# Feed-forward tiles of 1024 tokens in three passes, where they had 512 tokens in two

## The chip, the cores and the metric

One core of a Trainium2 chip. The time is the device time of one execution of the whole program, in microseconds; three executions are shown and their median counts.

## What is computed

A transformer block on 64 x 128 = 8192 tokens of width 512, all in float32.

```
x = x + tanh(g_xattn) * attention(layernorm(x), ctx, ctx)      # 32 query heads, 8 key heads, per batch of 128 tokens
n = layernorm(x)
shared = (silu(n @ Wsg) * (n @ Wsu)) @ Wsd * sigmoid(n @ Wse)  # 512 -> 1408 -> 512, every token
routed = for each of 32 experts: its first 64 tokens by top-4 choice,
         (silu(xe @ Wg) * (xe @ Wu)) @ Wd, weighted, added to their tokens   # 512 -> 352 -> 512
x = x + tanh(g_ffn) * (shared + routed)
```

## The kernel before

**Two stages.** The attention stage works through the 64 batches and writes the new rows to the output, the normalized rows and their transpose (`xT_dram`) to DRAM; beside that it prepares the first shared weights. The feed-forward stage, to which the change belongs, starts at 714.7 us in the profile and lasts to the end.

**Precision.** Every product of the shared part is made of three fast products: high x high, high x low, low x high (L1401 to L1403 and L1424 to L1426). So each operand exists as a rounded high part and a low part. ScalarE (ACT) writes the high part by a copy, VectorE (DVE) or GpSimd (POOL) the low part by a subtraction.

**Loops.** The 1408 hidden columns are 11 chunks of 128. They are covered in two passes over all tokens, of 5 and then 6 chunks (`NF`), since the split weights of one pass fill the memory that there is. A pass runs over 16 tiles of 512 tokens (`TILE`). A tile has a step for each chunk and then a down part.

**A step** multiplies both up projections of the chunk with the tile at once, by one level of a Strassen-Winograd scheme: seven products instead of eight, named by their operands (A11 B11, A12 B21, S4 B22, A22 T4, S2 T2, S1 T1, S3 T3). Each has two halves of depth and three precisions, so 42 matmuls per step, of 256 columns (`HT`, half a tile). They go to `p_a`, `p_b` and `p_c` in PSUM. ACT and DVE move and add the sums while TensorE (PE) goes on: ACT copies `p_a` and `p_c` to `term` and `sum16` (L1137, L1142, L1145); DVE adds them (L1357, L1319, L1364); ACT takes the silu (L1115); DVE multiplies the two halves of the tile (`h1`, L1322, and `h2`, L1325); ACT makes the high part `hh` (L1122) and DVE the low part `hl` (L1332). The last two products of a step, S4 B22 and A22 T4 (`last_two`, L1406), are issued inside the next step; those of the last step of a tile are issued inside the down part.

**The down part** (`down`, L1413) multiplies each block of 128 tokens with the down weights of the tile's chunks: three matmuls of 512 columns per chunk and block, into one of two banks of `acc`. DVE adds each finished block to its row of the output (`add_acc`, L1334). PE may write block j only when DVE has added block j - 2. Between these additions DVE prepares the next tile: four sums of its blocks (`x_sum`, L1189) and seven low parts (`x_low`, L1194), each over 512 elements per partition; ACT makes the seven high parts (`split_x`, L1100). The order in which PE takes the chunks of block 0 is written out by hand at L1479 to L1486: the last chunk's product has to wait for the whole chain from A22 T4 to `hl`, and other products are put ahead of it.

**Experts.** The 32 experts are done in 16 pairs, one pair beside one tile: gather of the rows (POOL), four transposes, 32 matmuls for gate and up, three transposes (L1466), six matmuls (L1473). The results are added to the output rows by gather, addition (L1284) and scatter, for each of the two halves; this may begin when the rows of the tile before have been stored (L1061), and the rows of the running tile may be loaded only after it (L957).

**Queues.** SP issues all plain loads and stores in the order of the program; its waits hold up what is behind them. Each engine works in the order of its code.

```
 31 NF = (5, 6)
 35 TILE = 512
1476 end = T.nf - 1
1480 down(T, 0, range(0, 2))
1481 last_two(T, end)
1482 down(T, 0, range(2, end))
1484 down(T, 1, range(0, 2))
1485 down(T, 0, range(end, T.nf))
1486 down(T, 1, range(2, T.nf))
```

## Time and profile before

| | us |
|---|---|
| median of 3 executions (2277.85 to 2278.27) | 2277.96 |
| the profiled execution | 2276.01 |
| its span, first to last instruction | 2274.2 |
| busy: PE / DVE / ACT / POOL | 2192.4 / 1539.9 / 1178.4 / 651.8 |
| feed-forward stage, first shared product to last | 714.7 to 2271.0 |
| granted TensorE clock, mean | 0.994 |

A matmul on PE overlaps the next one, so its duration in a row is longer than the time that it takes from the engine. What counts is the distance from start to start. A wait shows as a gap, or as a longer distance. In the rows, `chosen` also holds `gate`, `act_g`, `sum16`, `up2` and `eo`, since these share its memory, `x_raw` also holds the four sums, and `top` holds `xeT` and `y0`.

### The profile page before, as it was taken

How to read it: one execution, taken by the hardware profiler on the slowest of the kernel's cores; microseconds unless marked ns; L12 is line 12 of the kernel's file. 1: busy time of each engine (PE TensorE's matmuls, PEld its weight loads, DVE VectorE, ACT ScalarE, POOL GpSimd, SP SyncE). 2: the span in 40 equal slices, each digit the busy share in tenths (PEclk: the TensorE clock that was granted, in tenths of full speed). 3: DMA queues.
4: the chain of work that ended last, by engine and by line, in shares of the span. 5: the costliest groups of instructions: out<-in, count | busy, mean ns of one | idle time of the engine just before them, and what ended most of it. 6: DMA issues, size and time to landing. Idle time of an engine off the chain costs nothing. (4 is left out here: it accounts for less than half of the span.)

```text
span 2274.2 us, 53961 instructions
## 1 busy us (share of the span) xinstructions
PE 2192.4 (96%) x17121; PEld 1842.6 (81%) x17121; DVE 1539.9 (68%) x3135; ACT 1178.4 (52%) x2363; POOL 651.8 (29%) x1553
## 2 busy tenths in 40 slices
PE   6999999999997999999999999899999999999999
PEld 4777777777775888988889888798988989888888
DVE  6999999999996886556556556665555545455554
ACT  5888888888885433333333343433333333333332
POOL 5777777777773100000000003200000100001000
PEclk9999999999998999999999999999999999999999
DMA  3555555555554213443434435324243334344431
GB/s 82 144 141 139 147 142 134 147 143 136 143 151 125 68 65 129 147 147 110 143 120 138 141 116 174 130 96 137 84 138 92 115 101 137 98 153 157 155 104 65
DMA packets 318827, 286.25 MB, mean 126 GB/s; under 512 B 123265, under 2 KB 236929, under 8 KB 318722
## 3 DMA queue, kind: packets, MB, share of 16 engines
q1 hardware_dynamic: 314370, 272.23, 39.5%
q0 software_dynamic: 4352, 12.65, 2.1%
q8 instruction: 62, 1.02, 0.2%
q14 instruction: 43, 0.35, 0.1%
HBM read 195.43 MB, written 88.34 MB: 125 GB/s over the span
## 5 line engine op out<-in xcount | busy, mean ns | idle before, releaser
L1401 PE MATMUL p_a<-x_h,ws_h 128*128 128x256 f32 x1280 | 377.2, 295 | 17.3 <-ACT term L1137 10.1
L1402 PE MATMUL p_a<-x_l,ws_h 128*128 128x256 f32 x1280 | 363.0, 284 | 0.0
L1403 PE MATMUL p_a<-x_h,ws_l 128*128 128x256 f32 x1280 | 362.7, 283 | 0.0
L1115 ACT ACTIVATE chosen<-chosen 128x256 f32<-128x256 f32 x352 | 146.3, 417 | 394.2 <-DVE chosen L1319 213.0
L595 DVE TENSOR_REDUCE negmax<-p_max 128x8 f32<-128x1024 f32 x256 | 312.7, 1221 | 46.6 <-PE p_max L747 42.6
L1424 PE MATMUL acc<-wd_h,hh 128*128 128x512 f32 x704 | 277.0, 393 | 4.1 <-DVE rows L1339 3.3
L1401 PEld LDWEIGHTS p_a<-x_h,ws_h 128*128 128x128 f32 x1280 | 245.0, 191 | 38.5 <-ACT term L1137 14.2
L473 ACT ACTIVATE probs<-p_exp 128x1024 f32<-128x1024 f32 x256 | 261.3, 1021 | 27.2 <-PE p_exp L697 20.9
L1425 PE MATMUL acc<-wd_l,hh 128*128 128x512 f32 x704 | 274.9, 390 | 0.0
L1426 PE MATMUL acc<-wd_h,hl 128*128 128x512 f32 x704 | 274.5, 390 | 0.0
L1357 DVE TENSOR_TENSOR chosen<-p_b,term 128x256 f32<-128x256 f32 x176 | 74.7, 424 | 254.3 <-PE p_b L1403 153.1
L1402 PEld LDWEIGHTS p_a<-x_l,ws_h 128*128 128x128 f32 x1280 | 245.7, 192 | 0.6
L1403 PEld LDWEIGHTS p_a<-x_h,ws_l 128*128 128x128 f32 x1280 | 245.6, 192 | 0.0
L1047 POOL COPY cur_idx<-slot_idx 128x1 uint32 (+1 forms) x16 | 3.7, 230 | 708.7 <-DVE cur_w L1303 594.8
L1108 ACT ACTIVATE x_h<-x_raw 128x512 fp32r<-128x512 f32 x221 | 121.9, 619 | 154.4 <-DVE x_raw L1191 149.2
L747 PE MATMUL p_max<-kt,qt 128*128 128x256 f32 x1024 | 184.5, 302 | 1.9 <-DVE negmax L595 1.9
L1364 DVE TENSOR_TENSOR chosen<-p_a,term 128x256 f32<-128x256 f32 x176 | 74.4, 423 | 162.9 <-PE p_a L1403 161.6
L1401 PE MATMUL p_c<-x_h,ws_h 128*128 128x256 f32 x640 | 184.4, 288 | 0.0
L1402 PE MATMUL p_c<-x_l,ws_h 128*128 128x256 f32 x640 | 181.9, 284 | 0.0
L1403 PE MATMUL p_c<-x_h,ws_l 128*128 128x256 f32 x640 | 181.6, 284 | 0.0
L1137 ACT ACTIVATE term<-p_a 128x256 f32<-128x256 f32 x176 | 66.0, 375 | 203.4 <-PE p_a L1403 200.8
L1424 PEld LDWEIGHTS acc<-wd_h,hh 128*128 128x128 f32 x704 | 132.3, 188 | 42.1 <-issue 8.1
(199 smaller groups left out, 5378.4 us busy)
## 6 DMA issues: line engine op xcount, KB each, us to landing
rows<-out_dram SPq DMA_DIRECT2D x32, 1024.0 KB, 6.4
x_raw<-xn_cols SPq DMA_DIRECT2D x124, 256.0 KB, 2.9
out_dram<-rows SPq DMA_DIRECT2D x31, 1024.0 KB, 4.3
ew<-in_L_ffn_Wg_dram SPq DMA_DIRECT2D x32, 704.0 KB, 6.2
ew<-in_L_ffn_Wu_dram SPq DMA_DIRECT2D x32, 704.0 KB, 7.5
xs<-in_x_dram SPq DMA_DIRECT2D x64, 256.0 KB, 2.7
xres<-in_x_dram SPq DMA_DIRECT2D x64, 256.0 KB, 2.9
out_dram<-x SPq DMA_DIRECT2D x64, 256.0 KB, 2.6
```

Of the source, the lines that this page charges most:

```text
L473: nc.scalar.activation(probs[c][:, :], p_exp[:, :, :].rearrange("p a b -> p (a b)"), ACT.Exp, scale=float(D) ** -0.5).then_inc(exp_done, 1)
L595: nc.vector.tensor_reduce(negmax[c // 2][:, :].rearrange("p (g c i) -> p c i g", g=2, c=2)[:, c % 2, :, :], p_max[:, :, :].rearrange("p a ...
L747: last = mm(p_max[:, i // 2, 256 * (i % 2):256 * (i % 2) + 256], qt[B.par][:, c, 128 * i:128 * i + 128], kt[B.par][:, c, :], start=True, s ...
L1108: nc.scalar.activation(x_h[:, k, :, :], block(k), ACT.Copy).then_inc(xhi_done, 1)
L1115: nc.scalar.activation(act_g[:, cols], gate[:, cols], ACT.Silu).then_inc(silu2_done if half else silu1_done, 1)
L1357: nc.vector.tensor_tensor(gate[:, 0:HT], p_b[:, 0:HT], term[:, :], ALU.add).then_inc(c11_done, 1)
L1401: mm(bank, w_h[:, a, k, :], x_h[:, b, k, :], start=start and k == 0, stop=False, skip_group_check=not start)
L1402: mm(bank, w_h[:, a, k, :], x_l[:, b, k, :], start=False, stop=False, skip_group_check=not start)
L1403: last = mm(bank, w_l[:, a, k, :], x_h[:, b, k, :], start=False, stop=(k == 1), skip_group_check=not start)
L1424: mm(bank, hh[:, f, t], wd_h[:, d, :], start=(f == 0), stop=False)
L1425: mm(bank, hh[:, f, t], wd_l[:, d, :], start=False, stop=False)
L1426: last = mm(bank, hl[:, f, t], wd_h[:, d, :], start=False, stop=(f == T.nf - 1))
```

## The change

The tile becomes 1024 tokens, so a pass has 8 tiles, and the shared products have 512 columns. Twice the columns leave room for the split weights of at most 4 chunks, so the 11 chunks are covered in three passes of 4, 4 and 3. The extra chunk buffer `w5` goes. What is per tile (loads of the tile, its sums and its high and low parts, the expert pair's place) now comes 24 times over 1024 tokens where it came 32 times over 512. A tile's down part has 8 blocks instead of 4; the output rows pass through a ring of four blocks, each loaded, added and stored by itself. An expert pair stands beside every tile from the fourth to the nineteenth; its gate and its up weights now share one buffer, so that up is loaded when gate has been used. The preparation of the next pass's weights now happens at two changes of pass. The routing steps, one per step before, come two per step in the first three tiles. In the attention stage the prepared weights have 512 columns instead of 640.

```diff
-NF = (5, 6)
+NF = (4, 4, 3)
-TILE = 512
+TILE = 1024
+RB = 4
-        rows = sb("rows", [128, TB, E])
+        rows = sb("rows", [128, RB, E])
...
             def tiles(eng, body):
+                def one(part, i, pair=True, adds=True):
+                    p = NT * part + i - FIRST_P
+                    body(Tile(part, i), p if pair else None, p - 1 if adds else None)
...
 SP
+                    for j in range(TB):
+                        sp.wait_ge(add_done, TB * T.n + j + 1)
+                        sp.dma_start(row_block(T.i, j), rows[:, j % RB, :]).then_inc(rows_out[j % RB], 16)
+                        if 0 < j <= TB - RB:
+                            sp.wait_ge(rows_out[j - 1], 32 * T.n + 16)
+                            load_rows(T, j + RB - 1)
+                        if j == 5 and p is not None and not (isinstance(p, int) and p == NPAIR - 1):
+                            sp.wait_ge(ed_mm, p + 1)
+                            load_expert(p + 1, Wg, eg_in)
...
 ACT
-                        if T.at(0, 1) and f == 0:
-                            wide_high(0)
-                            down_high(NF[0])
...
+                        if T.ends and not T.last:
+                            if f == T.nf - 2:
+                                wide_high(T.part + 1, 0)
+                            if f == T.nf - 1:
+                                wide_high(T.part + 1, 1)
...
 DVE
-                    add_acc(T, 0)
-                    n = T.n + 1
-                    if not T.last:
-                        dve.wait_ge(xb_in, 32 * (T.n + 1))
-                        dve.wait_ge(xa_in, 32 * (T.n + 1))
-                        two_sums(n, low_block, low_block(T1))
-                        x_low(n, 0, low_block)
-                        four_sums(n, low_block)
-                    add_acc(T, 1)
-                    if not T.last:
-                        for j in range(1, NX):
-                            x_low(n, j, low_block)
-                    add_acc(T, 2)
-                    add_acc(T, 3)
+                    for j in range(TB):
+                        add_acc(T, j)
+                        if j == 4 and p is not None:
+                            scale_rows(p)
+                        if T.last:
+                            continue
+                        if j == 0:
+                            dve.wait_ge(xb_in, 32 * (n + 1))
+                            dve.wait_ge(xa_in, 32 * n)
+                            two_sums(n, low_block, low_block(T1))
+                        if j == 1:
+                            x_low(n, 0, low_block)
+                            x_sum(n, 3, T2, low_block(B22), low_block(T1))
+                        if j == 2:
+                            x_sum(n, 4, T4, low_block(B21), low_block(T2))
+                        if j > 1:
+                            x_low(n, j - 1, low_block)
...
 PE
                     down(T, 0, range(0, 2))
                     last_two(T, end)
+                    if p is not None:
+                        pe.wait_ge(eh_done, p + 1)
+                        for c, (a, n) in enumerate(FEC):
+                            last = tr(p_y[0:n, 128 * c:128 * c + 128], eh[:, a:a + n], ident[:, :])
+                        last.then_inc(ehT_mm, 1)
                     down(T, 0, range(2, end))
```

The order of the instructions at two places. **PE, the down part of a tile**, from the last matmul of A22 T4 to the first that waits for the last chunk's `hl`. Before, in the second pass (6 chunks), where the lines left out are twelve more of the same three:

```order
L1403 MATMUL p_a<-x_h,ws_l 128x256
L1424 MATMUL acc<-wd_h,hh 128x512 [waits hl_done]
L1425 MATMUL acc<-wd_l,hh 128x512
...
L1426 MATMUL acc<-wd_h,hl 128x512
L1424 MATMUL acc<-wd_h,hh 128x512 [waits hl_done]
```

Now, in the third pass (3 chunks), whole:

```order
L1414 MATMUL p_a<-x_h,ws_l 128x512
L1433 MATMUL acc<-wd_h,hh 128x512 [waits add_done]
L1434 MATMUL acc<-wd_l,hh 128x512
L1435 MATMUL acc<-wd_h,hl 128x512
L1433 MATMUL acc<-wd_h,hh 128x512
L1434 MATMUL acc<-wd_l,hh 128x512
L1435 MATMUL acc<-wd_h,hl 128x512
L1433 MATMUL acc<-wd_h,hh 128x512 [waits hl_done]
```

Between the two stand the products of two chunks where those of five stood (four in the first pass); with four chunks it is three.

**DVE, the end of a tile**, from the last `hl` on. Before:

```order
L1332 TENSOR_TENSOR hl<-chosen,hh 128x512
L1339 SCALAR_TENSOR_TENSOR rows<-acc,cur_g,rows 128x512
L1191 TENSOR_TENSOR x_raw<-x_raw 128x512 x2
L1198 TENSOR_TENSOR x_l<-x_raw,x_h 128x512
L1191 TENSOR_TENSOR x_raw<-x_raw 128x512 x2
L1339 SCALAR_TENSOR_TENSOR rows<-acc,cur_g,rows 128x512
L1198 TENSOR_TENSOR x_l<-x_raw,x_h 128x512 x6
L1339 SCALAR_TENSOR_TENSOR rows<-acc,cur_g,rows 128x512 x2
```

Now, up to the fourth of the eight additions:

```order
L1341 SCALAR_TENSOR_TENSOR rows<-acc,cur_g,rows 128x512
L1192 TENSOR_TENSOR x_raw<-x_raw 128x1024 x2
L1341 SCALAR_TENSOR_TENSOR rows<-acc,cur_g,rows 128x512
L1199 TENSOR_TENSOR x_l<-x_raw,x_h 128x1024
L1192 TENSOR_TENSOR x_raw<-x_raw 128x1024
L1341 SCALAR_TENSOR_TENSOR rows<-acc,cur_g,rows 128x512
L1192 TENSOR_TENSOR x_raw<-x_raw 128x1024
L1199 TENSOR_TENSOR x_l<-x_raw,x_h 128x1024
L1341 SCALAR_TENSOR_TENSOR rows<-acc,cur_g,rows 128x512
```

Each of the first four additions now has sums or low parts of twice the width between itself and the next.

## Rows read from the trace of the kernel before

**Rows 1.** The page, section 1: busy us, share of the span, instructions.
```profile
PE 2192.4 (96%) x17121; PEld 1842.6 (81%) x17121; DVE 1539.9 (68%) x3135; ACT 1178.4 (52%) x2363; POOL 651.8 (29%) x1553
```

**Rows 2.** Busy time by tile: stretch, length, engines, granted clock, DMA share, GB/s.
```profile
1205.99:1245.61 39.62, 39.48 (x271) 36.61 (x270) 23.95 (x50) 15.95 (x37) 3.79 (x4) 1.00 0.29 93
1158.16:1205.99 47.83, 47.83 (x322) 40.36 (x321) 25.33 (x55) 17.56 (x41) 1.99 (x4) 1.00 0.47 162
714.70:764.37 49.67, 43.48 (x273) 39.53 (x271) 36.51 (x66) 24.38 (x54) 10.15 (x12) 0.92 0.32 80
...
1380.60:1427.12 46.52, 41.77 (x272) 37.82 (x271) 29.17 (x47) 17.65 (x38) 23.11 (x23) 0.96 0.45 137
1427.12:1488.73 61.61, 57.58 (x376) 47.79 (x375) 40.02 (x67) 28.12 (x56) 10.47 (x11) 1.00 0.44 148
```

**Rows 3.** PE in order of time: start us, duration, line, operands, columns.
```profile
1200.28 0.39 PE L1426 MATMUL acc<-wd_h,hl 128*128 128x512 f32 x1
1200.51 0.39 PE L1424 MATMUL acc<-wd_h,hh 128*128 128x512 f32 x1
...
1206.11 0.28 PE L1402 MATMUL p_a<-x_l,ws_h 128*128 128x256 f32 x1
1206.23 0.28 PE L1403 MATMUL p_a<-x_h,ws_l 128*128 128x256 f32 x1
```

**Rows 4.** All engines in order of time, end of a tile of five chunks.
```profile
1233.27 0.40 PE L1424 MATMUL acc<-wd_h,hh 128*128 128x512 f32 x1
...
1233.47 0.42 DVE L1322 TENSOR_TENSOR chosen<-p_a,chosen 128x256 f32<-128x256 f32 x1 [0.29 <-PE p_a L1403]
...
1234.27 0.63 ACT L1122 ACTIVATE hh<-chosen 128x512 fp32r<-128x512 f32 x1 [0.63 <-DVE chosen L1325]
...
1234.93 0.69 DVE L1332 TENSOR_TENSOR hl<-chosen,hh 128x512 fp32r<-128x512 f32 x1 [0.70 <-ACT hh L1122]
...
1236.02 0.39 PE L1424 MATMUL acc<-wd_h,hh 128*128 128x512 f32 x1
```

**Rows 5.** DVE and ACT by shape in the feed-forward stage: count, busy us, mean ns.
```profile
L1332 DVE TENSOR_TENSOR hl<-chosen,hh 128x512 fp32r<-128x512 f32 x176 | 121.1, 688 | 22.3 <-ACT hh L1122 22.3
...
L1213 DVE TENSOR_TENSOR ws_l<-ws_raw,ws_h 128x1792 fp32r<-128x1792 f32 x5 | 10.2, 2046 | 0.3 <-ACT ws_h L1098 0.3
...
L1122 ACT ACTIVATE hh<-chosen 128x512 fp32r<-128x512 f32 x176 | 109.9, 624 | 24.2 <-DVE chosen L1325 24.2
...
L1098 ACT ACTIVATE ws_h<-ws_raw 128x1792 fp32r<-128x1792 f32 x5 | 8.4, 1684 | 0.0
```

**Rows 6.** DVE in order of time, same tile's additions and preparation of the next.
```profile
1237.00 0.75 DVE L1339 SCALAR_TENSOR_TENSOR rows<-acc,cur_g,rows 128x512 f32<-128x512 f32 x1 [1.38 <-PE acc L1426]
1237.67 1.41 DVE L1191 TENSOR_TENSOR x_raw<-x_raw 128x512 f32<-128x512 f32 x2
...
1241.93 3.69 DVE L1198 TENSOR_TENSOR x_l<-x_raw,x_h 128x512 fp32r<-128x512 f32 x6
```

**Rows 7.** PE's waits in the feed-forward stage: us in total, times, longest.
```profile
PE p_a L1401 <- ACT term L1137: 10.1, 14, 4.1
```

**Rows 8.** ACT in order of time, first tile: the copy that PE waits for.
```profile
720.40 0.40 ACT L1137 ACTIVATE term<-p_a 128x256 f32<-128x256 f32 x1
```

**Rows 9.** DVE in order of time, change of pass, while POOL forms weight sums.
```profile
1423.42 6.43 DVE L1198 TENSOR_TENSOR x_l<-x_raw,x_h 128x512 fp32r<-128x512 f32 x6
```

**Rows 10.** Granted clock around a stop of PE: the seventh number is the clock.
```profile
1391.00:1394.70 3.70, 1.56 (x11) 1.15 (x10) 1.61 (x3) 0.57 (x2) 0.69 (x1) 1.00 0.15 46
1394.70:1398.10 3.40, 3.23 (x15) 3.23 (x16) 1.51 (x4) 1.18 (x4) 0.30 (x2) 0.50 0.53 161
...
1421.00:1424.00 3.00, 0.76 (x4) 0.40 (x3) 2.93 (x4) 2.38 (x5) 2.76 (x4) 1.00 0.00 0
```

**Rows 11.** POOL in order of time: the gathers of a pair's two halves.
```profile
1212.43 0.97 POOL L1064 DMA_INDIRECT chosen<-out_dram,cur_tok  x1 [22.10 <-DMA out_dram<-rows]
...
1220.58 0.95 POOL L1064 DMA_INDIRECT chosen<-out_dram,cur_tok  x1 [2.53 <-DMA out_dram<-chosen,cur_tok]
```

More of the change, by code:

```diff
@@ L859, in tiles @@
+            FIRST_P = 3
             def tiles(eng, body):
-                def two(part, m, p):
-                    for j in range(2):
-                        t = Tile(part, 2 * m + j)
-                        t.flip = j * t.nf % 2
-                        pair = Pair(p, 0, 1, 2, 4) if j == 0 and p is not None else None
-                        body(t, pair, p if j == 1 else None)
-                two(0, 0, None)
-                two(0, 1, None)
-                two(0, 2, 0)
-                with eng.Fori(3, NT // 2 - 1) as m:
-                    two(0, m, m - 2)
@@ new lines, in tiles @@
+                one(0, FIRST_P, True, False)
+                with eng.Fori(FIRST_P + 1, NT - 1) as i:
+                    one(0, i)
+                one(0, NT - 1)
+                one(1, 0)
+                with eng.Fori(1, NT - 1) as i:
+                    one(1, i)
+                one(1, NT - 1)
+                for i in range(3):
+                    one(2, i)
+                one(2, 3, False, True)
+                with eng.Fori(4, NT - 1) as i:
+                    one(2, i, False, False)
@@ L898, in low_block, with chunk, cols @@
+                one(2, NT - 1, False, False)
+            def chunk(part, f):
+                return sum(NF[:part]) + f
+            def cols(f):
+                return slice(128 * f, 128 * f + 128)
             def low_block(k):
@@ L939, in body @@
+                def body(T, p, adds):
                     end = T.step + T.nf
+                    change = T.ends and not T.last
                     if T.at(0, 0):
-                        for s in range(NF[0]):
-                            load_down(s, s)
+                        load_x(0, 0, 1, T1, xb_in)
+                        load_x(0, 1, 1, B22, xb_in)
+                        for f in range(NF[0]):
+                            load_down(f, f)
                         sp.wait_ge(zeros_set, 1)
@@ L995, in _ @@
+                    if change:
+                        for f in range(NF[T.part + 1]):
+                            load_down(f, chunk(T.part + 1, f))
+                    for q in range(RB):
+                        sp.wait_ge(rows_out[q], 32 * (T.n + 1))
+                    alone(sp, spare_s2)
                 tiles(sp, body)
@@ L1161, in body @@
-                        if pair and f == pair.xt:
-                            act.wait_ge(xeT_mm, pair.p + 1)
-                            wait(act, eo_done, 2 * pair.p - 1)
+                        if T.at(0, 0) and f < 2:
+                            down_high(0, 2 * f)
+                            down_high(0, 2 * f + 1)
+                        if T.starts and T.part > 0:
+                            if f == 0 and NF[T.part] > 3:
+                                wide_high(T.part, 3)
+                            for j in range(2 * f, min(2 * f + 2, NF[T.part])):
+                                down_high(T.part, j)
@@ new lines, in work @@
+                def work(T, f, p, adds):
+                    if T.part == 0 and isinstance(T.i, int) and T.i < FIRST_P:
+                        for n in range(2):
+                            route_step(2 * (T.step + f) + n)
+                    if T.starts and T.part > 0 and f == 1 and NF[T.part] > 3:
+                        wide_low(T.part, 3)
+                    if T.ends and not T.last and f == T.nf - 1:
+                        wide_low(T.part + 1, 0)
+                    if adds is not None and f == 0:
+                        add_rows(adds, 0, y0)
@@ L1389, in _ @@
+                    if T.ends and not T.last:
+                        wide_low(T.part + 1, 2)
                 tiles(dve, body)
```

451 lines of the change are left out of this document (203 added, 248 removed).

## The prediction

> **What bounds the kernel now.** I read the page's engine shares first. PE is busy 96% of the span, DVE 68% [rows 1], so PE bounds the kernel and the question is what each microsecond of PE is. The attention stage ends at 714.7 us and the feed-forward stage takes 1556.3 us (714.7 to 2271.0). In order of time, matmuls of 512 columns follow each other by 0.227 us (1200.28 to 1200.51) and those of 256 columns by 0.120 us (1206.11 to 1206.23; 0.1197 averaged over the stage) [rows 3]. Twice 0.1197 is 0.2394, so a matmul costs some 13 ns beside its columns.
>
> Then the table by tile. A tile of five chunks takes 39.62 us and one with an expert pair 47.83 us, so a pair costs 8.2 us of PE [rows 2]. The stage is then: shared up products 176 steps x 42 x 0.1197 = 884.8; down products 2112 x 0.2273 = 480.1; pairs 16 x 8.2 = 131.2; sum 1496. The rest, 60 us, is waiting. It is not spread evenly: the first tile needs 49.67 us where a plain one needs 39.62, and the two tiles around the change of pass 46.52 (7 too many) and 61.61 [rows 2] (a pair, and a sixth step of 5.03 + 2.73, make 55.6: 6 too many). A quiet tile waits 0.3 to 0.9 us.
>
> **Part 1, wider products.** 7392 matmuls of 256 columns become 3696 of 512. At 0.2273 each they take 840.1, which removes **44.7 us**. Down products (176 x 12 before, 88 x 24 now) and pairs stay as they are. The sum without waits is 1451.4.
>
> A rule speaks against this part. The row shows 13 ns per matmul beside the columns [rows 3]. The Trainium skill, "TensorE: Matmul & The Clock Gate", Part 1 (section "Wait — 56ns, not 53.3ns?"), has columns / 2.4 GHz plus about 2.5 ns for a warm array; by it halving the count would remove 3696 x 2.5 ns = 9 us, and the whole sum would come out 35 us higher. It is a rival below; the trace disagrees with it here.
>
> **Part 2, the chain at the end of each tile.** This is what the change spoils. After A22 T4 of the last chunk come `h1`, `h2` (DVE), `hh` (ACT), `hl` (DVE), and only then PE may take the last chunk of block 0. Counted from PE's next matmul at 1233.27 they start at +0.20, +0.55, +1.00, +1.66 and end at +2.35; PE gets there at +2.75, since four chunk products of 3 x 0.227 = 0.68 us lie between [rows 4]. No wait, with 0.4 us to spare. Now every link is twice as wide. DVE takes 688 ns for 512 and 2046 for 1792 elements, ACT 624 and 1684 [rows 5]: 1.06 and 0.83 ns per element. `h1` and `h2` of 512 occupy DVE 0.61 apart and last 0.69, `hh` of 1024 lasts 1.05, `hl` of 1024 1.23. With the same 0.03 between links `hl` ends at +3.84, and PE goes on at +3.9. The cover shrinks at the same time: three chunk products with 4 chunks (+2.05), two with 3 chunks (+1.36); where a pair stands, its transposes add 0.35. PE stops 1.85 (3 tiles, 4 chunks, no pair), 1.5 (13 with a pair), 2.5 (5 tiles of 3 chunks) and 2.2 (3 with a pair): 5.6 + 19.5 + 12.5 + 6.6 = **44 us**.
>
> With 3 chunks there is one more: PE takes chunks 0 and 1 of block 0 right after the last step's S3 T3, and `hl` of chunk 1 stands on DVE behind the addition that follows S3 T3. It is there at 0.2 + 0.61 + 1.23 = +2.04, PE at +0.68: 1.4 us, in the 5 tiles without a pair (the 2.3 us of the pair's up products cover it in the others): **7 us**.
>
> **Part 3, DVE between the additions.** PE may start block j when block j - 2 is added. Before, additions follow at 0.67, two sums take 1.41, six low parts 3.69 [rows 6]. For 1024 elements a sum is 1.24 and a low part 1.15. Block 0 is complete for DVE at +4.9. The first eight starts of additions are then +4.9, 8.05 (two sums between), 11.1 (a low part and a sum), 14.2 (the same), 16.0, 17.8. A block costs PE 2.05 us with 3 chunks, 2.73 with 4. With 3 chunks PE would be at blocks 2 to 5 by +5.3, 7.7, 10.85, 13.9 and finds them free at +5.7, 8.8, 11.85, 14.95: 3.55 us in each of the 4 such tiles without a pair (the last tile prepares nothing). A pair's six down matmuls (2.1 us) sit ahead of block 4 and hide most, while its two scalings on DVE (1.5 us) hold up block 7: 2.4 us in 3 tiles. With 4 chunks it is 0.85 in 3 tiles and 0.2 in 13. Together 14.2 + 7.2 + 2.6 + 2.6 = **27 us**.
>
> **Part 4, start, changes of pass, the rest.** PE's longest wait before, 4.1 us, is for ACT's first copy of `p_a` [rows 7], at 720.40 [rows 8]; it comes after seven high parts and the expert keys. With high parts of 1024 (0.97 apart), sums of 1.24 and low parts of 1.15 I get the copy at 727.0, done at 727.6, while two products of 1.36 from 714.7 keep PE until 717.4: 10 us of wait, and some 2 us at the lower clock, **12**, where the tile's excess over a quiet one was 10 with the routing included. Routing steps (2.3 us each, two per step) fill DVE's spare time; at the ends of the first three tiles I take **4**. A change of pass: three of four weight chunks are ready in time; one low part of 1792 elements (2.05) stands ahead of the first addition, and POOL's last sums slow DVE's preparation as before, where six low parts took 6.43 instead of 3.69 us [rows 6, 9]: 3.5 each, **7**, for the 13 of before. The small waits of a step (0.1 us when a copy is just in time) mostly go, as a product lasts 1.36 instead of 0.72 and the copy only 0.6 instead of 0.38; I keep **4**. What `w5` cost on POOL and ACT in the second tile is gone with the old waits.
>
> **Queues.** SP issues 8 row loads and 8 stores of 0.4 us per tile, 6.4 us of at least 45. The pair's chain starts when the last block is stored. A gather issues 8.15 us after the one before [rows 11], and the addition 3 us after its gather. The first gathered rows are at DVE some 7 us into the next tile and block it there; DVE's next result (`c22_done`) is wanted by PE at 11.3, three products into step 1. Bound: 0 to 3 us per pair, I take 0. Row and tile traffic grows by a half in the stage and the gate and up weights are loaded one after the other; with a DMA share of 0.29 to 0.47 [rows 2] I take 0, bound 0 to 10 us. In the attention stage weight pieces shrink from 40 to 32 columns: 0 to -4, I take -1.
>
> **Sum.** Waits 44 + 7 + 27 + 12 + 4 + 7 + 4 = 105 against 60. The stage takes 1451.4 + 105 = 1556.4, what it took before (1556.3). With the attention stage's -1 this is 2275 against the 2276.0 of the profiled execution, which lies 2 us under the median of 2278.0. I predict **2278 us**: gain and loss cancel. A measurement of this kernel can tell about 0.2% (4.6 us) from no change.
>
> **Rivals.**
> *Slower, the clock falls at the stops.* At 1391.0 to 1394.7 PE stopped for 1.9 and 0.4 us and the granted clock was 0.50 for the next 3.4 us, while a stop of 2.3 us at 1421 left it at 1.00 [rows 10]. The new stops of 1.85 to 2.5 us lie between. It decides if the stops of 2.2 and 2.5 us act as the one at 1391 did: then the eight 3-chunk tiles lose up to 3.4 / 2 = 1.7 us at each fall, partly hidden in DVE's pace, and with more waits behind them 8 to 20 us: 2286 to 2300. Against it: they may as well act as the one at 1421 did. Chance 0.2.
> *Slower, the pair's chain comes late.* If the stores queue behind the 1.4 MB of gate weights that SP puts ahead of them, the first gathered rows reach DVE at 11 instead of 7 us, and `c22_done` holds PE 1 to 2 us in 16 tiles: 2294 to 2310. For it: those loads and stores now share the end of the tile; against: 4 us of margin. Chance 0.13.
> *Faster, the waits are shorter than worked out.* Each sum of part 3 is a queue that I filled without overlap. If DVE passes wide operations on at 1 us instead of 1.15 to 1.24, part 3 falls to 15 and part 2 to 36, and with -3 in the attention stage the result is 2256 to 2270. Chance 0.25.
> *The change does not do what it says.* If what a matmul costs beyond 2.4 GHz grows with the columns from `x_h`, 512 columns take 0.239 us and nothing is gained: 2278 + 45 = 2323. The down products at 0.227 speak against it. Chance 0.02. The skill's 2.5 ns per matmul would land near it, at 2313.
> *Forecast:* 0.40, own range 2270 to 2286.
>
> **Numbers.** Range 2260 to 2301: it takes in most of the first three rivals. Faster than 2273.4: 0.34. Within 4.6 us: 0.28. Slower: 0.38.
>
> **What would show it.** Matmuls of `p_a` 0.227 apart. A gap before L1433 of 1.5 to 2.5 us in every tile, its releaser `hl` (L1334); with 3 chunks further gaps of about 1 us released by the additions (L1341). First tile: ACT's copy at 727. Tiles of about 62 us (4 chunks), 70 with a pair, and 52.5 with 3 chunks. If PE's gap at `hl` is under 1 us in 4-chunk tiles, part 2 is wrong; if granted clocks of 0.50 stand in the 3-chunk tiles, the first rival holds; gaps before A22 T4 in step 1, released by DVE L1367, would be the second.

## The result and the profile after

| | before | changed |
|---|---|---|
| median | 2277.90 us (4 executions) | 2314.66 us (4, 2313.52 to 2316.77) |
| ratio | | 1.0164, interval 1.0151 to 1.0176 |
| profiled execution, its span | 2276.01, 2274.2 | 2313.52, 2311.7 |
| feed-forward stage, first shared product to last | 714.7 to 2271.0 | 713.7 to 2308.4 |

The change makes the kernel slower by 1.64%, where I forecast no change; the median lies above the range (2260 to 2301). The attention stage is 1.0 us shorter, as forecast. The whole loss, 38 us, is in the feed-forward stage, which takes 1594.7 us in place of 1556.3.

The page of the changed kernel, section 1, beside [rows 1]: PE is busy 26 us less and has a smaller share of a longer span.

```profile
PE 2166.0 (94%) x13425; PEld 1633.9 (71%) x13425; DVE 1604.8 (69%) x2577; ACT 1141.5 (49%) x1780; POOL 656.3 (28%) x1556
```

Two rows of PE in order of time (start, duration, line). The shared products of 512 columns follow each other by 0.2273 us on average, as forecast: the gain of part 1 is there.

```profile
1000.38 0.39 PE L1413 MATMUL p_a<-x_l,ws_h 128*128 128x512 f32 x1
1000.60 0.39 PE L1414 MATMUL p_a<-x_h,ws_l 128*128 128x512 f32 x1
```

So the waits must have grown by more. Busy time by tile answers to [rows 2] (stretch, length, PE, PEld, DVE, ACT, POOL, granted clock, DMA share, GB/s): the first tile, a tile of four chunks with a pair, the one at the first change of pass, the three tiles with three chunks and a pair (16 to 18, counted from 0), and one with three chunks and none.

```profile
713.70:794.50 80.80, 65.98 (x267) 51.60 (x266) 62.20 (x71) 32.83 (x47) 5.87 (x7) 0.92 0.33 97
994.00:1065.10 71.10, 69.75 (x317) 52.74 (x315) 40.37 (x53) 24.04 (x35) 6.07 (x8) 1.00 0.50 161
1207.20:1281.50 74.30, 70.32 (x316) 52.52 (x315) 46.75 (x55) 28.81 (x38) 25.56 (x24) 1.00 0.59 183
1854.30:1915.50 61.20, 56.50 (x250) 41.21 (x249) 37.07 (x48) 21.59 (x32) 9.85 (x11) 0.97 0.59 192
1915.50:1982.20 66.70, 58.49 (x250) 41.04 (x249) 35.69 (x48) 20.02 (x29) 6.00 (x8) 0.95 0.53 171
1982.20:2046.90 64.70, 57.41 (x250) 40.71 (x249) 35.68 (x48) 20.02 (x29) 4.85 (x6) 0.97 0.52 172
2099.70:2152.70 53.00, 47.89 (x199) 37.78 (x199) 31.96 (x39) 18.65 (x25) 0.00 (x0) 0.97 0.37 119
```

Forecast were 70 with a pair and 52.5 with three chunks: the quiet tiles are 1.1 and 0.5 us over. The three tiles of three chunks with a pair were worth 57.8 each by the same terms (products 28.6, down 16.4, pair 8.2, stop 2.2, additions 2.4). They took 61.2, 66.7 and 64.7, 19 us more.

PE's waits in the stage (us in total, times, longest), beside [rows 7]:

```profile
PE acc L1433 <- DVE hl L1334: 47.1, 29, 2.4
PE p_a L1412 <- ACT term L1137: 15.7, 7, 10.5
PE acc L1433 <- DVE rows L1341: 14.1, 24, 1.2
PE p_x L1443 <- DMA ew<-in_L_ffn_Wu_dram: 10.3, 3, 4.5
PE p_a L1412 <- DVE up L1367: 2.9, 4, 1.1
```

The first line is the new stop at `hl`, in every tile (in the tiles of three chunks without a pair a second one, at chunk 1); the fourth was not in the sum.

The end of a tile of four chunks with a pair, all engines in order of time, beside [rows 4]:

```profile
1039.42 0.49 PE L1486 MATMUL p_y<-ident,ebuf 128*128 128x128 f32 x3
1039.62 0.69 DVE L1324 TENSOR_TENSOR chosen<-p_a,chosen 128x512 f32<-128x512 f32 x1 [0.67 <-PE p_a L1414]
...
1040.23 0.68 DVE L1327 TENSOR_TENSOR chosen<-up,chosen 128x512 f32<-128x512 f32 x1
...
1040.94 1.06 ACT L1122 ACTIVATE hh<-chosen 128x1024 fp32r<-128x1024 f32 x1 [1.33 <-DVE chosen L1327]
...
1042.03 1.23 DVE L1334 TENSOR_TENSOR hl<-chosen,hh 128x1024 fp32r<-128x1024 f32 x1 [1.12 <-ACT hh L1122]
...
1043.31 0.50 PE L1433 MATMUL acc<-wd_h,hh 128*128 128x512 f32 x1 [1.33 <-DVE hl L1334]
...
1043.65 0.39 PE L1434 MATMUL acc<-wd_l,hh 128*128 128x512 f32 x1
```

Counted from PE's next matmul at 1039.42, the links start at +0.20, +0.81, +1.52 and +2.61, and PE goes on at +3.89. The forecast was +3.9. The last two rows show what it lacked: the first matmul after a wait is followed after 0.34 us in place of 0.23.

**Where the waits went.** I took every distance between two starts on PE in the stage, less 0.2273 (after a shared or down product). Distances that exceed it by over 0.25 are put down to what ended just before and called gaps; the rest, the pieces, are summed. The pairs stand at their whole time less 131.2.

| wait, us | forecast | changed kernel |
|---|---|---|
| stops at `hl` (last chunk 44, chunk 1 7) | 51 | 52.5, 31 gaps |
| DVE's additions, and the small pieces in the down parts | 27 | 43.3: 29 gaps of 19.6 in all, and 23.7 in pieces |
| up products: start 12, routing 4, changes of pass 7, small 4 | 27 | 30.4: 21.1 in gaps, 9.3 in pieces |
| the pairs' up weights | 0 | 10.7, 3 gaps |
| the pairs, over 8.2 each | 0 | 6.3 |
| sum | 105 | 143.2 |

The same table of the kernel before has pieces of 3.7 us in the down parts.

The second row holds two different things. Of its 43.3 us, waits that end with an addition make 22, the short ones among the pieces included. Another 17 us are no waits: they are the longer distances right behind a wait, or where PE passes from one kind of product to another, 151 in all (24 of them, 2 us, in the kernel before). The remaining 4 us are small spread and a few products at the slower clock. In the tile shown above, at block 3, both stand beside each other, 0.18 us of wait (0.41 less 0.23) and 0.11 us behind it:

```profile
1047.98 0.39 PE L1435 MATMUL acc<-wd_h,hl 128*128 128x512 f32 x1
1048.39 0.50 PE L1433 MATMUL acc<-wd_h,hh 128*128 128x512 f32 x1
1048.72 0.40 PE L1434 MATMUL acc<-wd_l,hh 128*128 128x512 f32 x1
```

### The profile page after: what moved, and what is told of

The parts are those of the page before. It is cut to its first block, busy times and chain, and to the rows that moved or that the text cites. A ratio compares the mean times of both kernels' runs of the same rounds, so it can differ in the third digit from the quotient of the medians.

```text
span 2311.7 us, 45131 instructions
## 1 busy us (share of the span) xinstructions
PE 2166.0 (94%) x13425; PEld 1633.9 (71%) x13425; DVE 1604.8 (69%) x2577; ACT 1141.5 (49%) x1780; POOL 656.3 (28%) x1556
## 4 chain that ended last, share of the span: by engine, by line
PE 51%; DVE 8%; DMA 6%; issue 3%; ACT 1%; SPq 1%; POOL 0%; DVEq 0%; POOLq 0%; ACTq 0%
PE acc L1433 7%; PE acc L1434 6%; PE acc L1435 6%; PE p_a L1412 5%; PE p_a L1414 5%; PE p_a L1413 5%; PE p_c L1412 3%; PE p_c L1413 3%; PE p_c L1414 3%; PE p_x L1443 2%; PE p_x L1502 2%; DVE hl L1334 2%; DMA eo<-out_dram,cur_tok 1%; DMA out_dram<-eo,cur_tok 1%; PE p_b L1412 1%
## 5 line engine op out<-in xcount | busy, mean ns | idle before, releaser
L1412 PE MATMUL p_a<-x_h,ws_h 128*128 128x512 f32 x704 | 279.7, 397 | 18.6 <-ACT term L1137 15.7
L474 ACT ACTIVATE probs<-p_exp 128x1024 f32<-128x1024 f32 x256 | 262.1, 1024 | 27.2 <-PE p_exp L698 21.0
L1414 PE MATMUL p_a<-x_h,ws_l 128*128 128x512 f32 x704 | 275.2, 391 | 0.0
L1413 PE MATMUL p_a<-x_l,ws_h 128*128 128x512 f32 x704 | 275.1, 391 | 0.0
L1108 ACT ACTIVATE x_h<-x_raw 128x1024 fp32r<-128x1024 f32 x166 | 162.3, 1046 | 159.6 <-DVE x_raw L1192 159.6
L1199 DVE TENSOR_TENSOR x_l<-x_raw,x_h 128x1024 fp32r<-128x1024 f32 x166 | 202.5, 1222 | 2.4
L1341 DVE SCALAR_TENSOR_TENSOR rows<-acc,cur_g,rows 128x512 f32<-128x512 f32 x192 | 143.8, 750 | 73.3 <-PE acc L1435 68.0
L698 PE MATMUL p_exp<-qt,kt 128*128 128x512 f32 x512 | 163.8, 401 | 0.1
L657 PE MATMUL p_tq<-ident,qs 128*128 128x128 f32 x1024 | 158.3, 278 | 2.6 <-POOL qs L378 1.8
L1435 PEld LDWEIGHTS acc<-wd_h,hl 128*128 128x128 f32 x704 | 133.4, 190 | 29.5
L458 ACT ACTIVATE qt<-p_tq 128x512 fp32r<-128x512 f32 x256 | 151.0, 590 | 6.3 <-PE p_tq L657 4.8
```

What stands on the lines that cost most here:

```text
L474: nc.scalar.activation(probs[c][:, :], p_exp[:, :, :].rearrange("p a b -> p (a b)"), ACT.Exp, scale=float(D) ** -0.5).then_inc(exp_done, 1)
L698: last = mm(p_exp[:, g2, :], kt[b.par][:, c, 128 * g2:128 * g2 + 128], qt[b.par][:, c, :], start=True, stop=True)
L1108: nc.scalar.activation(x_h[:, k, :, :], block(k), ACT.Copy).then_inc(xhi_done, 1)
L1199: nc.vector.tensor_tensor(x_l[:, k, :, :], block(k), x_h[:, k, :, :].bitcast(F32), ALU.subtract).then_inc(xlo_done, 1)
L1412: mm(bank, w_h[:, a, k, :], x_h[:, b, k, :], start=start and k == 0, stop=False, skip_group_check=not start)
L1413: mm(bank, w_h[:, a, k, :], x_l[:, b, k, :], start=False, stop=False, skip_group_check=not start)
```

## The experiments

Every run stands beside runs of the kernel before on its own chip, so ratios are compared. Theories: the loss is (A) the chain behind the last product, (B) DVE's program order, in which an addition stands behind the x preparation, (C) the transfers of the three tiles with three chunks and a pair, and the width gains what the distances say.

### The changed kernel again

> The changed kernel itself beside the others, so that the edits are compared on one chip: ratio 1.015 to 1.018 to the kernel before, as in its first measurement (1.0164).

Measured: 2311.85 us, ratio 1.0163 (1.0146 to 1.0180), as before. Its three tiles 16 to 18 took 61.5, 64.7 and 62.7 us, 3.7 us less together than in the first profile: they vary from one execution to another, while ten quiet tiles of four chunks with a pair take 71.05 to 71.09 each in this profile.

### split_cols: only the wider products undone

```
- mm(bank, w_h[:, a, k, :], x_h[:, b, k, :], ...)
+ for t in (slice(0, 256), slice(256, 512)):
+     mm(bank[:, t], w_h[:, a, k, :], x_h[:, b, k, t], ...)
```

> The only edit to the changed kernel: each 512-column product of the feed-forward stage is issued as two 256-column halves into the same bank, with the same weights one after the other; order, tiles, chunks and transfers stay. It undoes the wider products alone. Theory 1 (a product costs about 13 ns beside its columns, and the 3,696 wide products come at 0.227 us in place of two at 0.120): 3696 x (0.2394 - 0.2273) = +45 us, 2359 us, less what the later product ends give the chains: 2350 to 2362. Theory 2 (the width gained nothing, the same columns take the same time): within 3 us of 2314.7. By the Trainium skill, page TensorE: Matmul & The Clock Gate, section 'Wait — 56ns, not 53.3ns?', the fixed cost is some 2.5 ns, so that the halves would add about 9 us.

Measured: 2347.74 us, ratio 1.0324 (1.0307 to 1.0341). PE's rows in order of time:

```profile
1000.01 0.28 PE L1415 MATMUL p_a<-x_h,ws_l 128*128 128x256 f32 x1
1000.13 0.28 PE L1413 MATMUL p_a<-x_h,ws_h 128*128 128x256 f32 x1
```

The stage takes 31.9 us more: 44.7 in products less 13 in waits, since slower products cover more of what PE waits for. So the width is worth 32 to 37 us, and all the rest of the change (tiles of 1024, three passes, the ring) costs some 73 us (3.2%). Theory 1 holds, 2 us under its range. The Trainium skill, "TensorE: Matmul & The Clock Gate", section "Wait — 56ns, not 53.3ns?", has about 2.5 ns per matmul beside its columns; by an estimate from that figure it would have been 9 us. The trace disagrees: here a product pays 13 ns beside its columns.

### block1: more cover for the stop of four-chunk tiles

```
- down(T, 1, range(0, 2))
+ down(T, 1, range(0, end))
  down(T, 0, range(end, T.nf))
- down(T, 1, range(2, T.nf))
+ down(T, 1, range(end, T.nf))
```

> The only edit to the changed kernel: at the end of a tile token block 1 takes its products of all chunks but the last before block 0 takes its last chunk; with four chunks that moves one chunk's down products of 0.68 us (of some 0.23 us for each of three) between the last up product and the stop on h_l; with three chunks nothing moves. Theory 1 (every tile of four chunks stops TensorE at the last chunk's h_l because the chain of sigmoid, product, h_h and h_l takes longer than the down products put in its shadow): the stop of 1.49 us shrinks to 0.8 in 15 tiles and by as much in the first one, about 11 us in all: 2302 to 2306 us. Theory 2 (the stop is given back, since the additions of DVE behind it set the pace of the tail): the waits of the accumulation banks grow by as much: 2313 to 2316.

Measured: 2312.11 us, ratio 1.0161 (1.0144 to 1.0178): nothing. The stop did shrink, from 1.49 to 0.81 us, yet the tile still takes 71.1. PE's waits in the stage:

```profile
PE acc L1433 <- DVE hl L1334: 36.3, 29, 2.4
PE acc L1433 <- DVE rows L1341: 16.8, 37, 0.9
```

DVE in order of time, in the tile shown above:

```profile
1043.80 0.75 DVE L1341 SCALAR_TENSOR_TENSOR rows<-acc,cur_g,rows 128x512 f32<-128x512 f32 x1 [1.07 <-PE acc L1435]
1044.47 2.48 DVE L1192 TENSOR_TENSOR x_raw<-x_raw 128x1024 f32<-128x1024 f32 x2
1047.07 0.75 DVE L1341 SCALAR_TENSOR_TENSOR rows<-acc,cur_g,rows 128x512 f32<-128x512 f32 x1
```

PE finished block 1 0.7 us after block 0, but its addition comes 3.3 us after the other, behind two x sums. PE waits for its bank, 0.31 us at block 2 and 0.41 at block 3 (none and 0.18 in the changed kernel), and 0.11 more at each restart. Theory 2 holds: PE's block 3 waits for DVE's second addition, and that one stands the same time behind the chain as before. Behind the chain stands DVE's order, and both must go.

### two_first: every down product of two blocks behind the last product

```
- down(T, 0, range(0, 2))
  last_two(T, end)
  ...
- down(T, 0, range(2, end)); down(T, 1, range(0, 2))
+ down(T, 0, range(0, end)); down(T, 1, range(0, end))
  down(T, 0, range(end, T.nf))
- down(T, 1, range(2, T.nf))
+ down(T, 1, range(end, T.nf))
```

> The only edit to the changed kernel: at the end of a tile the second product group of the last chunk goes ahead of every down product instead of behind those of block 0's first two chunks; then blocks 0 and 1 take all chunks but the last, then both the last. The whole work of two token blocks on the chunks before lies in the shadow of the last chunk's chain. Theory 1 (the chain behind the last product, 2.9 to 3.8 us from PE's last up product to h_l, sets when the tail may go on): the stop of four-chunk tiles (1.49 us, 16 of them) goes, that of three-chunk tiles falls from 2.5 to about 1.2 (8 of them), and the stop of 1.4 us on chunk 1's h_l in the three-chunk tiles goes, since down products no longer come ahead of it: -42 to -47, so 2267 to 2273 us. Theory 2 (the pace of DVE's additions, one of about 0.7 us for each block, takes up what the stops give): -10 to -20, 2295 to 2305, with longer waits of the banks on rows.

Measured: 2285.84 us, ratio 1.0044 (1.0027 to 1.0060), 27 us less than the changed kernel. PE's waits in the stage:

```profile
PE acc L1433 <- DVE rows L1341: 28.2, 52, 2.1
...
PE acc L1433 <- DVE hl L1334: 7.1, 8, 1.0
```

DVE in order of time at the end of the same tile as above,

```profile
1044.41 2.48 DVE L1192 TENSOR_TENSOR x_raw<-x_raw 128x1024 f32<-128x1024 f32 x2 [0.62 <-DMA x_raw<-xn_cols]
1047.02 0.75 DVE L1341 SCALAR_TENSOR_TENSOR rows<-acc,cur_g,rows 128x512 f32<-128x512 f32 x1
```

and PE's start of the block behind that addition:

```profile
1047.82 0.50 PE L1433 MATMUL acc<-wd_h,hh 128*128 128x512 f32 x1 [0.96 <-DVE rows L1341]
```

Waits on `hl` fall by 40 us, as theory 1 said, and waits on additions rise by 14, as theory 2 said. The kernel's time lies between their ranges, 13 us above the first and 9 under the second. Besides, the x columns now arrive after the first addition, and DVE waits 0.62 us for them with the next addition behind.

### three: a third accumulation bank

```
- bank = acc[:, j % 2, :]
+ bank = (acc[:, 0, :], acc[:, 1, :], p_b[:, :])[j % 3]
- pe.wait_ge(add_done, TB * T.n + j - 1)
+ pe.wait_ge(add_done, TB * T.n + j - 2)
```

(blocks 0 to 2 take their last chunk after `hl`; the order is otherwise that of two_first. Since `p_b` also takes up products, PE waits for the sum that reads it before block 2, and for the last addition from it before the next tile's up product.)

> The changed kernel with the order of the run two_first at the end of a tile and a third accumulation bank for the down products (block j in bank j modulo 3; the third is p_b, free by then), so that TensorE may start block j when block j - 3 is added, where it had to wait for block j - 2. Theory 1 (what two_first did not win, and what block1 gave back, is the queue of DVE: an addition stands in program order behind two x sums of 1.24 us each or a low part of 1.2, so with two banks PE waits for it once or more per tile): the stops on rows of 0.5 to 1.1 us in the tiles with 4 chunks and of 0.8 to 1.1 us, three per tile, in those with 3 go: 25 us less than two_first, 2258 to 2264 us by the clock of this chip, ratio 0.990 to 0.997 to the kernel before. Theory 2 (DVE as a whole is the pace of the tail, its 8 additions and 12 x operations taking as long as PE's down products): the waits move to the next tile's first products, which want x_h and x_l, and the gain is under 10 us: ratio 1.000 to 1.004.

Measured: 2265.96 us, ratio 0.9945 (0.9929 to 0.9962): faster than the kernel before. Tiles of three chunks without a pair take 48.1 us where the changed kernel has 53.0. The waits on additions are 8.9 us in all, 28.2 in two_first, and the last 7.1 us on `hl` are gone too, since block 2 now stands in the chain's shadow as well; the run does not tell apart what the bank and what this cover is worth. What is late next is `up` (6.0 us in two_first). PE's waits in the stage:

```profile
PE p_a L1412 <- DVE up L1367: 20.9, 18, 3.8
...
PE acc L1433 <- DVE rows L1341: 5.8, 8, 0.8
PE p_b L1433 <- DVE rows L1341: 3.1, 4, 0.8
```

Theory 1 holds: the ratio is in its range, and 23 us are won where it had 25. Of what the additions gave back, a part went to that new wait: 16 of its 20.9 us stand where a pair's addition is ahead of the sum, the rest in the first three tiles.

### three_adds: the pair's additions behind PE's next sum

```
- if adds is not None and f == 0:
-     add_rows(adds, 0, y0)
- if adds is not None and f == 1:
-     add_rows(adds, 1, y1)
...
  nc.vector.tensor_tensor(up2, bank, term[:, :], ALU.add).then_inc(c22_done, 1)
+ if adds is not None and f < 2:
+     add_rows(adds, f, (y0, y1)[f])
```

> The run three with one more edit on DVE: the two additions of an expert pair's rows stand behind the second up sum of steps 0 and 1 of the next tile, where they stood ahead of it. In three PE waits 20.9 us in all, 18 times, for p_a <- DVE up, and DVE stands idle 7.6 to 7.7 us before each first addition, for the gathered rows. Theory 1 (DVE, blocked by the addition, holds the sum that PE's next product wants; with the stops at the tile's end gone this is the next wait in line): most of the 20.9 us go, 12 to 18 us less than three, ratio 0.986 to 0.990. Theory 2 (the chain of gather, addition, scatter is itself what the next tile's row and weight loads wait for, so that a later addition delays them): the gain is under 5 us, with longer waits for up weights in tiles 16 to 18, ratio 0.992 to 0.996.

Measured: 2259.69 us, ratio 0.9928 (0.9912 to 0.9945). DVE in order of time in the run three: it stands before the pair's addition, and the sum that PE wants stands behind it.

```profile
1212.24 0.68 DVE L1283 TENSOR_TENSOR eo<-top,eo 64x512 f32<-64x512 f32 x1 [7.56 <-DMA eo<-out_dram,cur_tok]
1212.85 0.68 DVE L1367 TENSOR_TENSOR up<-p_a,term 128x512 f32<-128x512 f32 x1
```

In three_adds these 16 us are gone (what is left of the line stands in the first three tiles), but the stage is only 6.0 us shorter, and the ratio's interval overlaps that of three. PE's waits, where `term` had 17.9 us in three and the weights 7.8:

```profile
PE p_a L1410 <- ACT term L1137: 23.8, 10, 10.6
PE p_x L1441 <- DMA ew<-in_L_ffn_Wu_dram: 8.7, 3, 4.1
...
PE p_a L1410 <- DVE up L1363: 4.9, 2, 2.5
```

Most four-chunk tiles win 0.5 to 1.1 us each (69.1 now). Tiles 16 to 18 take 188.6 us together in place of 183.7, and their waits did not shrink. In tiles 17 and 18 PE had waited 3.9 and 3.4 us for `up`; now it waits 3.9 and 2.8 at the same product for ACT's `term`. ACT in order of time, in tile 17:

```profile
1904.27 0.60 ACT L1165 ACTIVATE top<-p_x 128x512 f32<-128x512 f32 x1 [8.10 <-DVE eo L1283]
1904.76 0.59 ACT L1137 ACTIVATE term<-p_a 128x512 f32<-128x512 f32 x1
```

ACT copies the next pair's transposed rows (L1165) only when the pair's addition is done, since they share memory, and the copy that PE wants stands behind. So the same late addition holds PE by a second path, which the edit left as it was. The time is in theory 2's range, but the weights, which it named, are waited for only 0.9 us longer. That the three tiles lost 4.9 us is little more than the 3.7 by which they differ between the two profiles of the changed kernel.

### up_first: the up weights ahead of the row loads

```
+ if p is not None:
+     sp.wait_ge(eg_mm, p + 1)
+     load_expert(p, Wu, eu_in)
  if adds is not None:
      sp.wait_ge(eo_out, 32 * (adds + 1))
  for j in range(RB):
      load_rows(T, j)
...
- if p is not None:
-     sp.wait_ge(eg_mm, p + 1)
-     load_expert(p, Wu, eu_in)
```

> The only edit to the changed kernel: SyncE's queue issues an expert's up weights ahead of its wait for the output rows of the tile before and ahead of the row loads, instead of behind them; the x columns stay last. Theory 1 (the up weights of the big pass change, late behind rows and in front of three 512 KB loads of x, hold TensorE at the first up product of the three tiles with 3 chunks and a pair): the waits p_x <- Wu of tiles 16, 17 and 18 (2.4, 4.7 and 3.6 us in the changed kernel) go, with part of the slow clock behind them: 2298 to 2303 us, against 2314.7, and the three tiles take 58 to 61 us each in place of 61.2, 66.7 and 64.7. Theory 2 (the loss in these tiles is the saturated DMA queues themselves, whatever the order of issue): the up weights land about as late, or the x columns do in their place: 2312 to 2316. Theory 3 (the loss is in the chain at the end of each tile and in its restarts alone): within 2 us of the changed kernel.

The reading behind it, from the changed kernel: SyncE's queue in order of time in tile 17,

```profile
1939.08 1.77 SPq L915 DMA_DIRECT2D rows<-out_dram  x4
1940.89 0.98 SPq L905 DMA_DIRECT2D ew<-in_L_ffn_Wu_dram  x2
1941.92 3.78 SPq L908 DMA_DIRECT2D x_raw<-xn_cols  x3
```

PE's stop in the same tile,

```profile
1949.85 1.44 PE L1443 MATMUL p_x<-ew,top 128*64 128x352 f32 x4 [4.55 <-DMA ew<-in_L_ffn_Wu_dram]
```

and busy time by stretch around it:

```profile
1939.00:1945.00 6.00, 6.00 (x28) 4.88 (x26) 2.76 (x8) 2.25 (x4) 0.93 (x2) 1.00 0.83 259
1945.00:1950.00 5.00, 0.45 (x4) 0.15 (x4) 1.82 (x2) 1.16 (x2) 0.55 (x3) 0.86 1.05 390
1950.00:1953.00 3.00, 3.00 (x12) 1.25 (x14) 0.00 (x0) 0.00 (x0) 0.00 (x0) 0.50 0.74 281
```

The 1.4 MB of up weights are issued behind 1 MB of rows and beside 1.5 MB of x columns; from 1945 to 1950 the queues are full (share 1.05, 390 GB/s) and PE stands still. Then its clock is at half speed.

Measured: 2311.95 us, ratio 1.0163 (1.0146 to 1.0180): nothing won. The wait for weights is gone. SyncE's queue in tile 17 now reads:

```profile
1944.16 1.77 SPq L915 DMA_DIRECT2D rows<-out_dram  x4
1945.97 1.66 SPq L908 DMA_DIRECT2D x_raw<-xn_cols  x3
```

and DVE behind the first addition:

```profile
1962.80 2.48 DVE L1192 TENSOR_TENSOR x_raw<-x_raw 128x1024 f32<-128x1024 f32 x2 [3.16 <-DMA x_raw<-xn_cols]
```

Counted from the start of the tile, rows and x columns are issued 3.3 and 2.2 us later than in the changed kernel. DVE waits for x with an addition behind, and PE waits 4.1 us for that addition. Theory 2 holds here; the kernel's time alone could not tell it from theory 3.

### small_up: a quarter of the up weights

```
+ part = slice(0, 1) if src is Wu else slice(0, KC)
- sp.dma_start(ein[:, h, :, :], src[2 * p + h]...)
+ sp.dma_start(ein[:, h, part, :], src[2 * p + h]...[:, part, :])
```

This kernel leaves out three quarters of the up weights, so its output is another one; only its time counts.

> The changed kernel, but the load of an expert pair's up weights brings one of its four row blocks of 128 (176 KB in place of 704 KB for each expert); the other three keep the gate weights that lie there, so the experts' part of the output is another one. All waits and issues stay. It takes 1.06 MB out of what the queues carry in each of the 16 tiles with a pair. Theory 1 (the queues are saturated at the end of the three tiles that have a pair and 3 chunks: the up weights are 2.4 to 4.7 us late, and in up_first, where they go first, the x columns are as late instead): the waits on ew and the slow clock behind them go, and the x columns come in time: 12 to 18 us less than the changed kernel, ratio 1.008 to 1.011. Theory 2 (the up weights are late because SyncE issues them late, behind its wait for the output rows of the tile before): they still land 2 us late, since the issue stays at its place: ratio 1.013 to 1.016.

Measured: 2299.86 us, ratio 1.0095 (1.0078 to 1.0112), 15 us less. Tiles 16 to 18 take 58.8, 61.0 and 59.9 us, 13.0 less together than in the first profile and 9.3 less than in the second, and their matmuls of the pairs take 8.36 us each, none of them at the slow clock. What is left of PE's wait for them, in these three tiles:

```profile
PE p_x L1444 <- DMA ew<-in_L_ffn_Wu_dram: 1.2, 2, 0.9
```

Theory 1 holds: the volume is what is late, though every issue stayed at its place.

### keys_late: the routing behind the first copy

```
- act.wait_ge(key_mm, 1)
- (the 4 key copies, the wait for dv_done, the 2 exponentials)
  ...
+ (the wait for dv_done and the 2 exponentials behind the first step's term copy,
+  the key copies behind its first silu)
```

> The changed kernel with one edit in the first tile: ACT takes the copy of the expert keys and the two exponentials of the routing behind the first step's first copy of p_a and its first silu, where they stood ahead of them. TensorE's longest stop (10.7 us at 728.5) ends with that first copy at 727.84; ACT had been waiting for DVE's route_start until 727.37. Theory 1 (the routing in front of the copy holds it): the copy comes 3.5 to 4 us earlier, and the kernel takes 4 to 6 us less (a part of the slow clock behind the stop goes too): ratio 1.0138 to 1.0147. Theory 2 (the copy waits for the two products, which wait for x_h and x_l, whose sums DVE can't start before the transfers land at 716.1): the copy moves by under 1 us, or the routing then ends later and delays the pairs: ratio 1.016 to 1.017.

Measured: 2312.43 us, ratio 1.0151 (1.0134 to 1.0168). ACT's copy, in order of time:

```profile
724.23 0.57 ACT L1131 ACTIVATE term<-p_a 128x512 f32<-128x512 f32 x1
```

It stood at 727.84. PE's stop falls from 10.5 to 8.0 us and the first tile from 80.8 to 78.2: the copy moved as theory 1 said, the gain is half its size. The ratio can't tell it from nothing, and in its profile tiles 16 to 18 were 3 us longer than in the first. So neither theory is shown for the kernel's time.

### all, and best

all is three, keys_late and up_first together; best is three_adds with keys_late.

> The edits of three, keys_late and up_first together: a candidate that may beat both kernels. If the edits add up: three at 0.990 to 0.997, 4 to 6 us from the late keys, and 0 to 10 us from the up weights now that the x columns have the longer tail before them: ratio 0.985 to 0.993. Rival: with the stops at the end of a tile gone the transfers of the next tile have less time, and the three tiles with a pair and 3 chunks and the changes of pass wait for x columns or weights instead: ratio 0.995 to 1.002.

> The run three_adds with the late keys and exponentials of keys_late in the first tile (the trace of keys_late had that tile 2.6 us shorter, its stop at 8.1 in place of 10.7 us, though its median did not show it). If the parts add up: 2 to 3 us less than three_adds, ratio 0.984 to 0.989, a version faster than both kernels. If keys_late's gain is given back in the routing: the same as three_adds.

all: 2268.86 us, ratio 0.9967 (0.9953 to 0.9981), no better than three and in the range of the rival. At the two changes of pass up_first puts the pair's weights ahead of the next pass's, and PE waits there 4.6 us (1.7 in three) and 3.5 (3.3) for a copy that stands on ACT behind the split of these weights.

best: 2254.96 us, ratio 0.9910 (0.9893 to 0.9927), 20 us less than the kernel before and 57 less than the changed one. It is above the forecast range (0.984 to 0.989), which hung on a larger gain from three_adds; it is 5 us under three_adds, with intervals that overlap. PE is busy 95% of its span.

So the larger tile was not wrong in itself; its tail kept an order that fitted the smaller one. The third bank and the other order were not tried in the kernel before, where the stop at `hl` is missing; so what they are worth there stays open, and with it whether the larger tile is better once both are well ordered.

## Why the prediction was wrong

**The steps that failed.** The mechanism of gain and loss was right, and so were its two large terms: 44.7 us for the width, 51 for the stops. Two terms stood at nothing and measured 17 and 14 us: the longer distance of the first matmul behind a wait or a change of product, and the transfers (10.7 us of waits for up weights and 3.5 of slower pair products behind them). With start and pairs, 3 us each, they make 37 of the 38 us by which the stage missed the forecast.

**Part 1, right.** 44.7 us of products went, shown by the distances and by split_cols. My rival "nothing gained" and the price of 2.5 ns fell.

**Part 2, right to 2 us.** 51 forecast, 52.5 found, and the whole chain within 0.02 us. But I took the stop as a loss by itself and did not say what stands behind it: block1 took 0.7 us off 16 of these stops and won nothing.

**Part 3, right in its waits; the term beside them was missing.** The starts are right (+4.9 and +8.05 forecast, 1044.32 and 1047.58 found, +4.9 and +8.16). PE's waits for additions make 22 us where I had 27: 0.18 us in a quiet tile of four chunks, where I had 0.2, and 2.1 to 3.4 in one of three chunks without a pair, where I had 3.55. What I had at nothing is what comes with a wait: I priced a wait at its length. In a quiet tile of four chunks the down part loses 0.9 us beside the stop at `hl`, and 0.7 of that are distances longer by 0.09 to 0.11, one or two each time PE restarts or passes from one kind of product to the other. Over the stage such distances make the 17 us above. The tile of before has such pieces only around its pair. No run changes the restarts alone; in block1, which adds waits, the pieces in the down parts grow from 23.7 to 26.8 us, and in three, which removes most of the waits, they fall to 11.4.

**Queues: "with a DMA share of 0.29 to 0.47 [rows 2] I take 0, bound 0 to 10 us".** The share was a mean over a tile. What counts is 10 us of it, in which pairs, rows and x columns are wanted together, and there it reached 1.05. The shorter tiles of three chunks with a pair are where this ends on PE: 10.7 us of waits, and about 3.5 us of pair products at the slower clock. small_up gives back 15 us over the whole kernel, 9 to 13 of them in these tiles; up_first shows that putting the weights first does not help. By the Trainium skill, "Perfetto Trace Analysis", section "Roofline", the 16 DMA engines of a core end at about 435 GB/s. The trace agrees: the 390 measured at a share of 1.05 are near that, and I should have held the tail's volume against it.

**Start and routing, 27 us against 30.4.** The copy stood at 727.84 where I had 727.0. The first tile took 80.8 us: its stop is 10.5, 17 products around it at the lower clock lose nearly 4 us where I had 2, and three waits inside its steps, while DVE has the routing, take 2.2. How much of these is the routing's was not tested. The two changes of pass were right: 3.2 and 3.8 us for 3.5 each.

**Pairs, 131.2 us against 137.5.** 2.6 us are from 8.36 in place of 8.2 us each, the rest is the clock.

**Rivals.** The clock did fall at the stops: in the three-chunk part five times. Yet most of that cost nothing. The granted clock of the changed kernel behind tile 16's stop at `hl`, a stretch of the same view as the tiles above:

```profile
1897.30:1900.70 3.40, 3.40 (x9) 2.35 (x8) 3.05 (x3) 0.16 (x1) 0.00 (x0) 0.52 0.21 79
```

This tile takes 61.2 us; in the repeat, at full speed, it waits 1.1 us more for additions and 0.4 more for weights, and takes 61.5. Tiles 20 and 22 with such a fall and tile 21 without take 53.0 each. DVE is the pace there, as the rival said in part. The pair's chain through `c22_done` cost 0.8 us in the changed kernel (the other 2.1 of that line are in the first three tiles, before any pair), but 16 once the tail was cured (three). I had its place right and its margin too large: the first addition stands 8.5 to 9.2 us into a quiet tile where I had 7, and 10.4 to 11.4 in three. The waits for additions were 5 us shorter than worked out, too little for the rival of shorter waits.

**The range.** All misses lie on one side, 16 in the row of the additions, 11 for the weights, 3 at the start, 6 in the pairs and 2 in part 2, and they make the 38 us. I had treated the terms as if their errors would offset each other.

## What to carry to other kernels

When the tile doubled, the engine with the most work gained at once, and each chain between engines doubled in length while its cover did not. So redo the order of the tile's end with the tile: first find what else PE can do in the chain's shadow, then whether it has a bank to do it in, then what the other engine runs between two results that PE wants. Give every new wait a price for the restart behind it, here 0.11 us. When you move an operation out of one wait, look for a second engine that also waits for it. Check transfers against the fullest 10 us, not the mean of a tile, and do not count on terms that you set to nothing to offset each other.

## What the runs showed that I had not expected

- A matmul started after a wait is followed 0.34 us later, where a running one is followed after 0.23 (1043.31 to 1043.65): 0.11 us, beside the wait itself. With the changes between kinds of products that was 17 us in the down parts.
- A granted clock of half speed can cost nothing: tile 16 took 61.2 us with it and 61.5 without. It did cost where pair products ran in it.
- Slower products hid 13 us of waits in split_cols, which is why the measured worth of the width (36 us) is less than that of its matmuls (44.7).
- The three tiles whose transfers are late together took 188.9 and 192.6 us in two profiles of one kernel, while ten quiet tiles of the second agree to 0.04 us.
- An addition moved behind the sum that PE wants still held PE as long, by way of ACT (three_adds, tiles 17 and 18).
